# Two-layer cross-attention kernel: row copies moved to ScalarE's queue, constant loads and context squares moved later, filler multiplies on TensorE

## The reference, cut to what matters

```python
# layer 0
sa = mha(x, x, ..., mask=band of 64, bias=slopes * (j - i)); x = layernorm(x + sa)   # stage 0
ca = mha(x, ctx, ...);                                    x = layernorm(x + ca)      # stage 1
ff = gelu(x @ w1 + b1) @ w2 + b2;                         x = layernorm(x + ff)
# layer 1
q = rmsnorm(x) * g_q @ Wq;  k, v = rmsnorm(ctx) * g_c @ Wk, Wv                       # stage 2
out = rmsnorm(x + softmax(q k^T * scale + mask) v @ Wo) * g_out
```

## Time and profile before

| what | value |
|---|---|
| three runs | 572.53, 572.91, 574.24 us; median 572.91 |
| the profiled execution | 571.68 us, its span 569.9 us |
| busy share of the span | TensorE 89%, VectorE 78%, ScalarE 75%, GpSimd 59% |
| mean granted clock of TensorE | 0.981 of full speed |
| DMA | 63.51 MB, mean 111 GB/s |

### The profile page before, as it was taken

One profiled execution on the slowest core, in us unless ns is written; L12 is line 12 of the kernel. 1 busy time (PEld: TensorE's weight loads), 2 busy tenths in 40 slices (PEclk: granted clock), 3 DMA queues, 4 the chain that ended last, 5 costly groups with the idle time before them and its releaser, 6 DMA issues.

```text
span 569.9 us, 17389 instructions
## 1 busy us (share of the span) xinstructions
PE 506.6 (89%) x6772; PEld 276.4 (49%) x6772; DVE 442.7 (78%) x911; ACT 427.1 (75%) x658; POOL 338.8 (59%) x640
## 2 busy tenths in 40 slices
PE   3577879877789999999999999999999999998984
PEld 2345556654434444455554545454545454444432
DVE  6335555646989999888889898989888999999912
ACT  3136666645367888989898989898898888787793
POOL 7344488883549627566576767675858384663032
PEclk9969999989989999999999999999999999999998
DMA  3957655564616347060615162425435361524000
GB/s 104 214 118 211 180 155 158 154 189 102 167 54 141 116 74 185 9 183 20 169 55 134 50 141 87 104 87 102 127 64 138 62 177 52 152 91 89 3 21 19
DMA packets 90195, 63.51 MB, mean 111 GB/s; under 512 B 6446, under 2 KB 89630, under 8 KB 90026
## 3 DMA queue, kind: packets, MB, share of 16 engines
q1 hardware_dynamic: 89540, 61.91, 42.0%
q10 hardware_dynamic: 574, 0.49, 0.5%
HBM read 34.99 MB, written 26.22 MB: 107 GB/s over the span
## 4 chain that ended last, share of the span: by engine, by line
PE 62%; DVE 8%; SPq 8%; ACT 7%; issue 6%; DMA 5%; POOL 4%; ACTq 0%; POOLq 0%; DVEq 0%
PE pv L646 20%; PE ps L627 11%; PE ps L582 10%; DVE negmax L945 6%; ACT probs L781 5%; PE ps L692 3%; PE ps L744 3%; PE ps L681 3%; PE ps L708 3%; DMA kst<-k_parts 2%; SPq L441 2%; PE ps L671 2%; PE ps L732 2%; SPq L466 2%; DMA qst<-mT 2%
## 5 line engine op out<-in xcount | busy, mean ns | idle before, releaser
L945 DVE TENSOR_REDUCE negmax<-ps 128x1 f32<-128x512 f32 x512 | 320.5, 683 | 25.7 <-PE ps L627 20.3
L781 ACT ACTIVATE probs<-ps 128x1024 f32<-128x1024 f32 x288 | 287.5, 1025 | 67.5 <-PE ps L582 40.5
L646 PE MATMUL pv<-probs,vp 128*32 128x256 f32 (+1 forms) x3072 | 158.6, 334 | 2.8 <-issue 2.8
L627 PE MATMUL ps<-kst,qst 61*128 61x512 bf16 x512 | 104.9, 385 | 8.5 <-DVE negmax L945 5.4
L582 PE MATMUL ps<-qst,kst 64*128 64x256 bf16 x1024 | 97.5, 273 | 6.5 <-ACT probs L781 3.1
L646 PEld LDWEIGHTS pv<-probs,vp 128*32 128x32 f32 x3072 | 70.4, 111 | 54.9 <-issue 28.1
L1056 POOL TENSOR_SCALAR mcap<-negmax 128x16 f32<-128x16 f32 x48 | 12.2, 254 | 107.4 <-DVE negmax L945 43.7
L582 PEld LDWEIGHTS ps<-qst,kst 64*128 64x128 bf16 x1024 | 38.7, 94 | 63.0 <-issue 21.8
L941 DVE TENSOR_REDUCE negmax<-ps 128x4 f32<-128x512 f32 x64 | 40.2, 684 | 27.5 <-PE ps L618 27.5
L627 PEld LDWEIGHTS ps<-kst,qst 61*128 61x128 bf16 x512 | 27.5, 93 | 58.9 <-DVE negmax L945 31.4
L1093 POOL TENSOR_TENSOR qr<-qf,qs 128x256 f32<-128x256 f32 x24 | 16.1, 670 | 58.2 <-ACT qs L805 31.3
(11 more groups left out here) (132 smaller groups left out, 762.8 us busy)
## 6 DMA issues: line engine op xcount, KB each, us to landing
kst<-k_parts SPq DMA_DIRECT2D x64, 192.0 KB, 4.3
qst<-q_parts SPq DMA_DIRECT2D x48, 192.0 KB, 3.8
k_parts<-ks SPq DMA_DIRECT2D x16, 384.0 KB, 2.7
q_parts<-qs SPq DMA_DIRECT2D x24, 192.0 KB, 2.2
cin<-in_ctx_dram SPq DMA_DIRECT2D x16, 256.0 KB, 3.0
k_parts<-ks SPq DMA_DIRECT2D x16, 256.0 KB, 3.1
q_parts<-qs SPq DMA_DIRECT2D x24, 128.0 KB, 2.3
k_parts<-ks SPq DMA_DIRECT2D x24, 128.0 KB, 3.2
```

The costliest lines, as they stand in the source:

```text
L627: mm = nc.tensor.matmul(empty_banks("X", u.index, n + g), q[rows_in(g, 0, ROW_M), four, tile * P:(tile + 1) * P], k[rows_in(g, 0, ROW_M), ...
L646: mm = nc.tensor.matmul(pv[32 * j:32 * j + 32, dst:dst + n], vp[u.parity][:, c, 4 * quad + j, :], probs[:, quad, src:src + n], start=(quad ...
L781: nc.scalar.activation(to, src, ACT.Exp, scale=SCALE).then_inc(act_emptied, 1)
L945: ins = nc.vector.tensor_reduce(negmax[:, tile, at:at + 1], src, AX.X, ALU.max, negate=True)
```

## The change

The copies of constant rows for stacks 1 and 2 are both issued by ScalarE, just ahead of its first `V` copy in step -1; SyncE no longer waits for them before `load_stacks` of units 0 to 2 (only for the memory fill). SyncE's loads of columns, constants and remaining weights move from step 0 to the end of step -1, behind the rows of maxima. `load_early` moves from the middle of SyncE's step to its end, behind `load_stacks`, and loads batch i in step i; the squares of batch i are taken in step i+1, so `C` leaves `FIRST_SELF` and comes into `FIRST_CROSS`; the `SELF` strings stay as they are. TensorE gets constant multiplies into `pv`: 56 before the first score tile for the maxima, 6 before each of the next three, 8 before the first score tile for the exponentials. VectorE prepares the weights of stages 1 and 2 at the start of step 2 and not in step 0. Two bank orders change, in steps 8 and 23.

```diff
-FIRST_SELF = ("XC:01 B3 raw V:1 Q:4 ... S:12 M0:6 C X:53 P1 B:5 P2 "
+FIRST_SELF = "XC:01 B3 raw V:1 Q:4 ... S:12 M0:6 X:53 P1 B:5 P2 O:0"
-               "S:23 X:45 S:01 P0b X:04 S:12 X:36 V:5 A:2 S:01 X:36 X:54 P1a ...
+               "S:23 X:45 S:01 P0b C X:04 S:12 X:36 V:5 A:2 X:36 S:01 X:54 P1a ...
-LAST_CROSS = ("S:45 S:01 B3 raw ...
+LAST_CROSS = ("S:45 S:12 B3 raw ...
...
-                yield "context", self.main, None, at
+                yield "context", self.before if 0 < self.i <= B else None, None, at
...
                 if n.index < STACKS:
-                    sp.wait_ge(stack_rows[n.stack], STACK_ROWS[n.stack])
+                    sp.wait_ge(stack_zeroed[n.stack], 2)
...
-                if s.i == 0:
-                    sp.dma_start(win[:, 3:9, :], a["w_in"][:, 3:9, :]).then_inc(win_rest, 16)
-                    sp.dma_start(cols[:, :], a["columns"]).then_inc(cols_loaded, 16)
-                    for dst, src in const_loads():
-                        sp.dma_start(dst, src).then_inc(consts_loaded, 16)
...
-                if s.main is not None and s.main.stage == 0:
-                    for batch in (0, 1) if s.i == 0 else (s.i + 1,):
-                        if batch < B:
-                            load_early(batch)
...
-                if s.i == -1:
-                    sp.wait_ge(ones_loaded, 64)
-                    sp.wait_ge(stack_zeroed[1], 2)
-                    copy_rows(sp, 1)
...
                 if s.nxt is not None:
                     load_maxima(s.nxt, 0)
+                if s.i == -1:
+                    sp.dma_start(cols[:, :], a["columns"]).then_inc(cols_loaded, 16)
+                    for dst, src in const_loads():
+                        sp.dma_start(dst, src).then_inc(consts_loaded, 16)
+                    sp.dma_start(win[:, 3:9, :], a["w_in"][:, 3:9, :]).then_inc(win_rest, 16)
                 if s.n is not None and not early:
                     load_stacks(s.n)
+                if s.main is not None and s.main.stage == 0:
+                    load_early(s.main.batch)
...
+            def idle(count):
+
+                pe.wait_ge(masks_loaded, 32)
+                for _ in range(count):
+                    nc.tensor.matmul(pv[:, 0:P], identb[:, :], band[:, :], start=True, stop=True, skip_group_check=True)
...
+                    if kind == "maxima" and u.index == 0:
+                        idle(56 if what == 0 else 6)
+                    if kind == "scores" and u.index == 0 and what == 0:
+                        idle(8)
...
+            def copy_constant_rows():
+                act.wait_ge(ones_loaded, 64)
+                act.wait_ge(stack_rows[0], STACK_ROWS[0])
+                for i in range(1, STACKS):
+                    act.wait_ge(stack_zeroed[i], 2)
+                    copy_rows(act, i)
...
-                if s.i == 0:
-                    act.wait_ge(ones_loaded, 64)
-                    act.wait_ge(stack_rows[0], STACK_ROWS[0])
-                    act.wait_ge(stack_zeroed[2], 2)
-                    copy_rows(act, 2)
...
+                        if what == "V" and u.index == 0:
+                            copy_constant_rows()
...
+            def bias_columns():
+                dve.wait_ge(cols_loaded, 16)
...
                 if s.i == 2:
+                    other_weights()
                     make_key_mask()
...
                         if what == "B":
-                            other_weights()
+                            bias_columns()
```

More of the change, by code:

```diff
@@ L73 @@
 SECOND_STEP = "XC:23 Q:0 K:2 X:45 X:64 V:0 M0:5 X:64 X:56"
-FIRST_SELF = ("XC:01 B3 raw V:1 Q:4 S:01 M1:5 X:32 K:1 S:12 X:30 X:26 D:5 A:5 S:45 P0 S:12 M0:6 C X:53 P1 B:5 P2 "
-              "O:0")
+FIRST_SELF = "XC:01 B3 raw V:1 Q:4 S:01 M1:5 X:32 K:1 S:12 X:30 X:26 D:5 A:5 S:45 P0 S:12 M0:6 X:53 P1 B:5 P2 O:0"
 SELF = "C B3 XC:56 V:0 raw Q:3 S:45 M1:1 D:0 K:1 X:43 S:56 X:21 P0 X:04 S:23 P1 A:5 M0:0 S:34 X:51 O:2 P2"
@@ L86 @@
 FIRST_CROSS = ("S:01 XC:34 B3 X:24 raw S:01 Q:5 X:36 X:16 S:23 M1:1 X:46 X:01 S:23 P0a sq X:64 X:05 S:23 T:5 K:1 D:6 "
-               "S:23 X:45 S:01 P0b X:04 S:12 X:36 V:5 A:2 S:01 X:36 X:54 P1a S:23 X:10 S:56 P1b X:12 S:34 P2a S:56 "
+               "S:23 X:45 S:01 P0b C X:04 S:12 X:36 V:5 A:2 X:36 S:01 X:54 P1a S:23 X:10 S:56 P1b X:12 S:34 P2a S:56 "
                "M0:2 X:34 O:0 S:12 P2b S:45 X:61 S:23 P3a")
-LAST_CROSS = ("S:45 S:01 B3 raw S:45 M1:2 S:23 S:45 P0a S:01 S:56 D:2 S:01 P0b S:56 S:34 S:01 S:56 P1 A:0 S:34 S:12 "
+LAST_CROSS = ("S:45 S:12 B3 raw S:45 M1:2 S:23 S:45 P0a S:01 S:56 D:2 S:01 P0b S:56 S:34 S:01 S:56 P1 A:0 S:34 S:12 "
               "S:56 P2 S:23 O:4 P3a")
@@ L916, in other_weights @@
                 weights_of(1)
-                dve.wait_ge(cols_loaded, 16)
                 weights_of(2)
                 nc.vector.tensor_scalar(w["v2"], win[:, 8, :], cols[:, 5:6], None, ALU.mult).then_inc(v_weights, 1)
+            def bias_columns():
+                dve.wait_ge(cols_loaded, 16)
                 dve.wait_ge(zero_set, 1)
```

## The result

The changed kernel took 608.38 us (median of 4 runs, 605.74 to 609.57) where the kernel before took 572.72 (4 runs). The ratio is 1.0617, 95% interval 1.0569 to 1.0666: some 35 us slower. The forecast was 611, range 594 to 624. The ratios here leave out slow executions and are not quotients of two medians, so the two can differ by about 1 us. The profiled execution has a span of 607.8 us, 37.9 more than before, and a mean granted clock of 0.932 of full speed where it was 0.981.

What follows compares the result with a forecast made beforehand. Stage 0 was taken as bound by a loop of latencies through ScalarE, TensorE, GpSimd and SyncE. Start -1, waits +28, clock +10 and step 7 +1 gave +38 on 571.68, 609.7, placed at 611 us, range 594 to 624.

Steps and rivals of the forecast that it cites:

- The place and the mechanism: Stage 0, steps 1 to 5: ScalarE waits at the squares for the later context load, paid anew every turn; +28 us.
- up to step 1's XC copy: Start until XC is copied in step 1: earlier maxima nearly all spent at the first squares; -1 us, bounds -4 to +2.
- four turns, the wait itself: Steps 1 to 5, ScalarE before the squares: 7.0 us a turn for four turns, +28 us, bounds +26 to +34.
- four turns, the clock: TensorE at half clock behind the squares' waits: 2.0 us a step, +8 us of the +10 for five steps.
- step 5's clock, step 7's wait: Half clock in step 5, +2 us, and ScalarE's wait for the context at step 7's squares, +1 us.
- the start: SyncE before the first maxima: row-copy wait removed, 3.9 us for unit 1's stores, maxima 2.8 us earlier; net -1 us.
- Rival 1: Steps 1 to 5: clock doesn't fall or ScalarE's copies hide it, only the +28 us stays; 601 us, chance 0.15.
- Rival 2: Squares' wait in stage 0 is paid once, later steps have slack; about 581 us, chance 0.07.
- Rival 3: Context lands before ScalarE reaches the squares, so the start's gain stays: 567.4 us, chance 0.07.
- Rival 4: TensorE at half clock through whole steps, +17 us for the clock, landings near 4.9 us; 625 us, chance 0.07.
- the fillers alone would decide: Start, TensorE: by the clock page's rule, fillers give full rate in the first 25 us; no separate chance given.

Runs made afterwards that it cites:

- Experiment 1: Changed kernel with the squares moved behind P0 in the step lists (steps 1 to 5 and 7), all else as changed: 567.67 us, ratio 0.9954 to the kernel before.
- experiment 4: Changed kernel with the squares still first, but their context load issued ahead of the stack loads: 590.43 us, ratio 1.0334 to the kernel before.
- experiment 3: Kernel before with only the squares' part added (load behind the stack loads, squares a step later, first in SELF): 610.77 us, ratio 1.0717.
- experiment 5: Changed kernel with 96 constant multiplies ahead of the Q projection in each of steps 1 to 5: 606.71 us, ratio 1.0644 to the kernel before.
- experiment 7: Changed kernel with squares behind P0 and the x load for batches 3 to 7 behind the first rows of maxima: 567.97 us, ratio 0.9965.
- experiment 2: Changed kernel with the squares' load and step put back as before, all other edits kept: 568.89 us, ratio 0.9952 to the kernel before.
- experiment 6: Changed kernel with squares behind P0 and none of the 82 filler multiplies: 568.33 us, ratio 0.9933 to the kernel before.

## Why the prediction was right, and which terms were not

**The place and the mechanism were right.** The squares' load is issued behind the last stack load, ScalarE gets to the squares some us earlier, and the delay is paid in each turn. Experiment 1 takes it away by the squares' place, experiment 4 halves it by the load's place, experiment 3 makes it on the kernel before. The path from the squares to the next load was only partly as written. The prediction let the load follow from K, by GpSimd and SyncE's stores. From step 2 on it runs through the X tiles and the rows of maxima, which SyncE sends ahead of the stack loads, and K's stores are out by then.

**The terms**, against the span's 37.9 us:

| term | forecast | measured | from |
|---|---|---|---|
| up to step 1's XC copy | -1 (-4 to +2) | +5.2 | 54.80 + 0.35 against 49.93 |
| four turns, the wait itself | +28 (26 to 34) | +21.0 | 4 x (20.24 - 13.01) less the clock |
| four turns, the clock | +8 | +7.9 | 4 x (10.78 - 8.81), experiment 5 |
| step 5's clock, step 7's wait | +2 + 1 | +3.8 | all behind step 5's XC copy |
| sum | +38 | +37.9 | |

The sum was nearer than its terms: the start and the wait were mis-sized by 6 and by 7 us, with opposite signs. That they cancel is luck. The split of the turns into wait and clock rests on one execution of each kernel.

**The start** was mis-sized, and left its bounds. The step said that SyncE would wait 3.9 us for the stores of unit 1 and gain 2.8. The stores' landing was taken from a row in which the row copies came after them. In the changed kernel they go beside them, and landing took 7.72 us; the gain was 0. The copies alone don't explain it. With them beside the stores, but 640 KB of x moved away (experiment 7), the same store, the last of q, landed in 4.9 us; in the kernel before, with all of x ahead and the copies behind, in 4.8. Only both neighbours together made it 7.7. That a transfer's landing time belongs to its neighbours, and the copies move onto it, was written down only as the lower bound. The DMA engines' share over 18 to 22 us is 1.13 at 187 GB/s, where before it was 0.99 at 295 GB/s: the engines were full in both. The Trainium skill, page "DMA: Bandwidth & Descriptors", section "Issuing engines are not separate DMA queues", says that transfers issued by different engines run on the same DMA engines and interleave; the trace agrees. Changed, then before:

```profile
18.00:22.00 4.00, 2.75 (x49) 1.91 (x50) 1.79 (x3) 0.00 (x0) 0.00 (x0) 0.73 1.13 187
```

```profile
18.00:22.00 4.00, 2.81 (x43) 1.91 (x44) 1.92 (x4) 0.00 (x0) 0.00 (x0) 1.00 0.99 295
```

From there the count to 43.3 for the last stack issue was short by 5.5 (it was 48.82), 2.8 for the missing gain; the rest is near what TensorE's half clock from 34 on cost (experiment 1, at full clock there, was 3.0 us earlier at this point).

**The clock** came out as priced, 2.0 us a turn, but by other instructions. The prediction counted V (1.13 us, 2.05 at half clock) behind XC's copy. It and the text ahead of it let V wait for the copy of its own step. That is not so: V of a step belongs to unit i+1, whose XC was copied a step earlier (`unit_of` in the kernel says so). In the changed kernel it runs at 68.10, ahead of the wait, and the first to wait is Q.

```profile
68.10 1.06 PE L685 MATMUL ps<-win,xc 128*128 128x128 f32 x8
...
75.88 1.19 PE L669 MATMUL ps<-xc,w0q 128*128 128x256 f32 x2 [6.72 <-ACT xc L798]
```

Q at half clock stands on the chain in full, 1.19 us where experiment 5 has 0.70. With it the score tile, the transposes, K and the first X tiles run at half clock, and from Q to the first maxima that makes 1.8 of the 2.0 us. So with V off the path and the X tiles on it the size stayed where it was. That is luck too.

**The wait itself** was mis-sized: 7.0 us a turn were taken and 5.3 came (20.24 - 13.01 - 1.97). Landings were 3.2 to 3.6 us as taken, and the squares took 1.61 us. What was too long is the stretch from the end of the XC copy to the last stack issue. The rows of before have 14.8 us for it (49.93 to 64.76), and the prediction kept that and put the clock's 2.0 us on top. In the changed kernel it is 14.9 us with the half clock in it, so about 13 without. A part of the difference can be seen: SyncE took 2.34 us to issue the two reloads of q in step 4 of the kernel before (not in every step: 0.93 at 88.13) and 0.96 in the changed one. Before, then changed:

```profile
100.33 2.34 SPq L466 DMA_DIRECT2D qst<-q_parts  x2
```

```profile
67.17 0.96 SPq L465 DMA_DIRECT2D qst<-q_parts  x2
```

**Step 7** waited 3.81 us, not 1: its context load took 6.28 us to land (163.20 to 169.48), where 3.5 was taken.

**The rivals.** Rival 1 (+28 alone, 601) falls: the clock did fall, and the chain shows the slow multiplies on it, not hidden. That experiment 5's runs came out at 606.71 us, hardly under the changed kernel's 608.38, is the one thing left for it. Rival 2 falls: five waits of 6.4 to 8.3 us. Rival 3 needed the context to land before the squares; experiments 1 and 2 show that with the wait gone the kernel is 2.7 us faster, not 5.5. Rival 4 falls: in the turn shown the granted clock is back at 1.00 from 82 us on, some 6 us behind the wait. The Trainium skill, page "TensorE: Matmul & The Clock Gate", section "The HAM clock gate", says that activity lifts the half rate; the trace agrees in the turns (0.50 behind the wait, 1.00 after dense work). That the fillers alone would decide falls by experiment 6.

## What to carry to other kernels

A load and its user stand in two lists. Before moving either, put the issue time plus the landing beside the time at which the user's engine reaches it, in the same step; if the load's issue depends in turn on what stands behind the user, the difference is paid in every turn. The cheapest repair is often the user's place: here one token in two strings, worth some 38 us (ratio 1.0617 against 0.9954). The landing time of a transfer has to be taken with the neighbours that it will have after the change. And where two executions are held against each other to price one thing, cut the turn into stretches first: the net of 1.1 us hid a price of 2.0 and a loss of 0.9 elsewhere.

## What the runs showed of the hardware that was not expected

- The changed kernel and experiment 1 are the same program until the squares of step 1, some 45 us in, fillers included, and their first score tiles start at 33.31 and 33.20. Yet from 34 to 38 us the granted clock was 0.50 in one and 1.00 in the other, and unit 2's stack loads were issued 3.0 us apart (from 46.89 and from 43.91). Ahead of the first score tile TensorE had stood 2.35 us in the one and 0.94 in the other. First the changed kernel, then experiment 1:

```profile
34.00:38.00 4.00, 3.07 (x34) 1.40 (x30) 1.57 (x3) 1.86 (x3) 0.36 (x1) 0.50 0.97 349
```

```profile
34.00:38.00 4.00, 2.50 (x61) 1.41 (x60) 1.76 (x4) 2.49 (x4) 2.12 (x5) 1.00 0.97 342
```

 So part of the +5.2 us at the start is one execution's clock and not the change.
- The fillers cost 57.5 ns each at full clock (5.52 us for 96 of 128 x 128 in bf16, weights loaded each time). The 56 at the start took 4.34 us, 77 ns each, at a granted clock of 1.00 too; why isn't shown. 8 of them ahead of the wait of 2.35 us did not keep the clock up behind it.
